# Second attention of a two-layer macaron block: which step turns the first half of the outputs, and which steps give ScalarE both score pairs

## The chip, the cores and the metric

The kernel runs on one core of one Trainium2 chip. The metric is device time in microseconds, from launch to end, as the median of three runs. All engines named are those of this core: TensorE (matmuls), VectorE, ScalarE, GpSimd, and SyncE, whose queue issues the DMAs.

## What is computed

Eight sequences of 512 tokens, 128 channels, pass through two layers of (half FFN, attention, half FFN). The stages in order are ffn0, attn0, ffn0, ffn1, attn1, ffn1. The change touches attn1 alone. There, with 16 heads of 8 channels:

```
qkv = x @ w_qkv;  q, k, v per head
w = relu(q k^T / sqrt(8))
attn = (w / (sum(w) + 1e-6)) @ v
y = x + attn @ w_out + b_out
x_new = x_in + layernorm(y) * gamma + beta
```

(the x of this formula is itself the layer norm of the running x_in.)

## The kernel before

**Tiling.** A chunk is one sequence of 512 tokens; each stage runs over eight chunks. Each engine has its own instruction stream, written out by hand as tables of steps, and the streams meet in semaphores. A body of an attn1 chunk has sixteen steps (slots). In each step an engine first does its tail steps for the chunk before, then its prep steps for the chunk after, then its main work of this chunk. What comes earlier in this order is ahead in the engine's queue.

**Main work.** Step n of attn1 handles four heads (quad n // 4) against one block of 128 keys (n % 4). TensorE (pe_attn1) makes two score pairs, m = 2n and 2n + 1. Each is two matmuls of 128 keys by 512 queries into the double bank pair[m % 3] (L818). A score pair must be read out before pair m + 3 may be written (taken_wait). The read-out is the ReLU into the ring probs. Even pairs are always ScalarE's (L944). Odd pairs are VectorE's (L1227), except in the steps of ACT_BOTH, where ScalarE does both. Of the 32 pairs of a chunk ScalarE does 21 and VectorE 11.

**Products.** PV n (pv1, L646) multiplies the four heads' weights of step n with the values and adds to bank 6. PV_AT says in which step it is issued, behind the scores: PV 7 in step 9, none in step 10, PV 8 to 12 in steps 11 to 15, and the last three in steps 0 and 1 of the next chunk. PVs 0 to 7 fill the first half of the outputs and PVs 8 to 15 the second.

**Taking a half out.** take_half (VectorE, L1146 to L1158) waits until the eight products of the half are done, turns bank 6 (a 32x32 block transpose), adds the epsilon, takes the reciprocal and multiplies. PV 8 (and PV 0 of the next chunk) waits for the turn. The first half is taken at the head of the step HALF_AT["attn1"], ahead of that step's ReLU; the second in step 2 of the next chunk.

**Tail of an attn1 chunk, run during the next.** VectorE: second half in step 2, fin in step 3, aT_lo in step 5. TensorE: proj in step 10 (twelve matmuls on bank 7). VectorE: y_norm in step 11 (L1257 to L1266, it waits for proj). GpSimd: y_rstd in step 12 (L1291). VectorE: y_scale in step 13 (L1271). GpSimd: y_add in step 14 (L1295 and L1298).

**Preparation of the next chunk.** In step 15 GpSimd does keep (L1284). In step 0 VectorE takes the layer norm's statistics (ending with ve, L967) and GpSimd makes rstd (L1279). In step 1 VectorE makes xn (L976), ahead of ReLU 3. In step 3 TensorE transposes xn (L544). GpSimd also copies the values of a quad into place (put_values, L1315, steps 2, 9, 10 and 15) and adds the bias row in step 10 (L1321).

The first chunk of attn1 has the tail of an ffn1 chunk in place of proj to y_add, and the last one prepares an ffn1 chunk, with the router's steps on VectorE and ScalarE.

Of the kernel before, what the change touches and what calls it, by code (L numbers as in the profile page):

```python
# [117 lines left out]
NPAIR = 3  # L118
NP1 = 2 * NS1
PV_AT = ((-3,), (-2, -1), (), (0, 1), (2,), (3,), (4,), (5,), (6,), (7,), (), (8,), (9,), (10,), (11,), (12,))  # L120
ACT_BOTH = (0, 2, 10, 11, 13)
HALF_AT = {"attn0": 13, "attn1": 10}
PUT_AT = {"attn0": (11, 13, 18, 3), "attn1": (9, 10, 15, 2)}
Q_FILLS = ((0, ((3, 0),)), (1, ((3, 0),)), (0, ((2, 0), (0, 384))), (1, ((2, 0), (0, 384))), (None, ((1, 0),)))
K_FILLS = ((0, ((0, 0),)), (1, ((0, 0),)), (0, ((1, P), (3, 0))), (1, ((1, P), (3, 0))), (None, ((2, 0),)))
# [11 lines left out]
def ring(use):  # L137

    what, n = use
    return (USES.index((what, n % NS0)) - (len(USES) if n < 0 else 0)) % NPAIR  # L140
# [49 lines left out]
def taken_by(m):  # L190

    return "act" if m % 2 == 0 or m // 2 in ACT_BOTH else "dve"

# [6 lines left out]
def build(nc, x_in, w0, w1, wa, biases, bd3, rows, consts, out, scratch, mixed):  # L200
    nc.disable_value_cache = True
    ctx = ExitStack()
    with ctx:
# [930 lines left out]
        def take_half(eng, ch, half):  # L1134

            mem, n = ch.mem, 2 * ch.ga + half
            if ch.causal:
                eng.wait_ge(pv0_done, 3 * (NQ * ch.g + 2 * half + 2))
                src = bank6
            else:  # L1140
                eng.wait_ge(pv1_done, ROUND + ch.g * NS1 + (2 * half + 2) * NT)
                src = bank6
            eng.wait_ge(attn_ready, n)
            if ch.causal and half:
                eng.wait_ge(x_done, ONE + ch.G)
            eng.transpose(mem.o_turn[:, :, :].rearrange("p n c -> p (n c)"), src[:, :]).then_inc(o_turned, 1)  # L1146
            eng.wait_ge(o_turned, n + 1)
            o = mem.o_turn[:, :, 0:2 * VC].rearrange("p n (g c) -> p n g c", c=VC)
            if ch.causal:
                eng.reciprocal(rden[:, 1, :, :], o[:, :, :, HD]).then_inc(rden_ready, 1)  # L1150
            else:
                eng.tensor_scalar(rden[:, 0, :, :], o[:, :, :, HD], KERN_EPS, None, ALU.add).then_inc(eps_added, 1)
                eng.wait_ge(eps_added, 2 * ch.g + half + 1)
                eng.reciprocal(rden[:, 1, :, :], rden[:, 0, :, :]).then_inc(rden_ready, 1)
            eng.wait_ge(rden_ready, n + 1)
            if half == 0:
                eng.wait_ge(aT_ready, ch.ga)
            eng.tensor_tensor(  # L1158
                mem.attn[:, :, 16 * half:16 * half + 16].rearrange("p n (g d) -> p n g d", d=HD), o[:, :, :, 0:HD],
                rden[:, 1, :, :].unsqueeze(3).broadcast_to([P, NBLK, 2, HD]), ALU.mult).then_inc(attn_ready, 1)  # L1160
# [13 lines left out]
        def maximum(eng, ch, f, b):  # L1174

            quad, fill, m = f // NF, f % NF, mem0
            k = ch.g * NS0 + f + 1
            q = m.rmax[:, quad % 2, :, :]
            src = pair[b]
            eng.wait_ge(s_ready, k)  # L1180
            heads = slice(0, QUAD) if fill == NF - 1 else slice(2 * Q_FILLS[fill][0], 2 * Q_FILLS[fill][0] + 2)
            if fill == NF - 1:
                eng.tensor_reduce(q[:, 1, :].rearrange("p (h b) -> p b h", b=2), src[:, :, :].rearrange("p b (h s) -> p b h s", h=2),  # L1183
                                  AX_X, ALU.max).then_inc(s_used, 1)
            elif len(Q_FILLS[fill][1]) == 1:
                eng.tensor_reduce(q[:, 3, heads], src[:, :, :], AX_X, ALU.max).then_inc(s_used, 1)
            else:
                eng.tensor_reduce(q[:, 2, heads], src[:, :, 0:384], AX_X, ALU.max)
                eng.tensor_reduce(q[:, 0, heads], src[:, :, 384:S], AX_X, ALU.max).then_inc(s_used, 1)
            if fill == NF - 1:  # L1190
                st = neg_max
                st.begin(NQ * ch.g + quad)
                eng.wait_ge(s_used, k)
                eng.wait_ge(mx_zeroed, 1)
                if quad or not ch.first:
                    eng.wait_ge(q_ps, NQ * ch.g + quad)
                mx_hi, mx_lo = (mx[:, :, :].rearrange("p t (h r) -> p t h r", r=PC)[:, :, :, NROW * HD + i] for i in range(2))
                v = st.mark(eng.tensor_scalar(mx_hi, q, -1.0, None, ALU.mult))
                eng.wait_ge(st.sem, v)
                st.mark(eng.scalar_tensor_tensor(mx_lo, q, -1.0, mx_hi.bitcast(F32), ALU.mult, ALU.subtract))  # L1200
                st.end()

        def dve_attn0(eng, ch, n):
# [9 lines left out]
            elif not ch.last:  # L1213
                maximum(eng, ch.after(), f - NS0, ring(("q", n)))
            if n == HALF_AT["attn0"]:
                take_half(eng, ch, 0)

        def dve_attn1(eng, ch, n):

            i = ch.g * NS1 + n  # L1220
            if n == HALF_AT["attn1"]:
                take_half(eng, ch, 0)
# [493 lines left out]
```

## Time and profile before

| | us |
|---|---|
| median of 3 runs | 2091.01 (2084.22 to 2091.42) |
| profiled execution, its own time | 2088.05 |
| its span, first to last instruction | 2086.0 |
| attn1 in that span | about 1440 to 1702 |

| engine | busy us | share of the span |
|---|---|---|
| TensorE matmul | 1991.1 | 95% |
| TensorE weight load | 1440.4 | 69% |
| VectorE | 1646.3 | 79% |
| ScalarE | 1198.4 | 57% |
| GpSimd | 929.6 | 45% |

The mean granted clock of TensorE is 0.984 of full speed. Ends of matmuls are modelled, so a busy TensorE isn't one at its peak. In the rows, PE is TensorE, DVE VectorE, ACT ScalarE, POOL GpSimd, and L12 is line 12 of the kernel.

### The profile page before, as it was taken

What the parts mean: (1) busy time and instruction counts of PE and PEld (TensorE: products, weight loads), DVE (VectorE), ACT (ScalarE), POOL (GpSimd) and SP (SyncE); (2) the same over time, 40 slices, a digit from 0 to 9 for tenths busy, and PEclk for the clock granted to TensorE, in tenths of its full rate; (3) what the DMA queues carried; (4) which work ended last, traced back from release to release, by engine and by line L of the source; (5) the groups of instructions that cost most, each with busy time, mean ns of one, the idle gap of its engine ahead of it and who ended that gap; (6) DMA issues with size and microseconds to landing.
All of it is one profiled execution on the core that took longest, in us unless ns stands there. A gap on an engine that the chain in (4) does not pass through costs nothing.

```text
span 2086.0 us, 44742 instructions
## 1 busy us (share of the span) xinstructions
PE 1991.1 (95%) x10752; PEld 1440.4 (69%) x10752; DVE 1646.3 (79%) x3337; ACT 1198.4 (57%) x1736; POOL 929.6 (45%) x904
## 2 busy tenths in 40 slices
PE   6999998999999889999999999998999999999998
PEld 4777776666666677777777888885333347787787
DVE  6777787777777577777768888886777788888887
ACT  6667664555555657667644444444767764445444
POOL 4655553233333356666634444442222235444444
PEclk9999999999999999999999999999999999999999
DMA  5333333333323134444401111113342411111112
GB/s 203 99 117 111 101 119 113 97 97 98 93 80 91 45 110 127 114 126 126 125 26 43 50 50 41 46 46 110 113 131 81 131 37 45 47 42 46 41 51 71
DMA packets 120701, 179.29 MB, mean 86 GB/s; under 512 B 33840, under 2 KB 38576, under 8 KB 120496
## 3 DMA queue, kind: packets, MB, share of 16 engines
q1 hardware_dynamic: 120624, 178.37, 28.9%
q8 instruction: 36, 0.59, 0.1%
q14 instruction: 41, 0.34, 0.0%
HBM read 147.10 MB, written 31.20 MB: 85 GB/s over the span
## 4 chain that ended last, share of the span: by engine, by line
PE 61%; DVE 12%; issue 12%; POOL 9%; ACT 3%; DVEq 1%; DMA 1%; SPq 1%; POOLq 1%; ACTq 0%
PE pair L392 13%; PE pair L394 12%; PE pair L393 12%; POOL h_lo L1358 6%; PE bank L646 4%; PE pair L735 3%; PE bank L624 3%; PE pair L757 3%; PE pair L818 2%; PE bank L392 2%; PE bank L394 1%; PE bank L393 1%; DVE rmax L1183 1%; DVE xn L976 1%; DVE h_hi L1126 1%
## 5 line engine op out<-in xcount | busy, mean ns | idle before, releaser
L1364 POOL TENSOR_TENSOR h_lo<-hid,h_hi 128x512 fp32r<-128x512 f32 x256 | 335.5, 1311 | 409.6 <-ACT h_hi L915 409.4
L1358 POOL TENSOR_TENSOR h_lo<-hid,h_hi 128x512 fp32r<-128x512 f32 x256 | 331.5, 1297 | 216.3 <-ACT h_hi L881 215.7
L392 PE MATMUL pair<-xnT_hi,w_hi 128*128 (+1 forms) x1040 | 420.4, 404 | 4.4 <-DVE prod L1105 3.0
L394 PE MATMUL pair<-xnT_hi,w_lo 128*128 (+1 forms) x1040 | 408.0, 392 | 0.0
L393 PE MATMUL pair<-xnT_lo,w_hi 128*128 (+1 forms) x1040 | 407.2, 392 | 0.0
L910 ACT ACTIVATE hid<-pair,bias 128x512 f32<-128x512 f32 x256 | 176.5, 689 | 315.7 <-PE pair L394 275.2
L392 PE MATMUL pair<-h_hi,w_hi 128*128 128x512 f32 x784 | 312.0, 398 | 14.4 <-DVE h_lo L1128 6.3
L394 PE MATMUL pair<-h_hi,w_lo 128*128 128x512 f32 x784 | 306.4, 391 | 0.0
L393 PE MATMUL pair<-h_lo,w_hi 128*128 128x512 f32 x784 | 306.2, 391 | 0.0
L1126 DVE TENSOR_SCALAR h_hi<-pair,nb 128x512 fp32r<-128x512 f32 x256 | 191.1, 746 | 70.3 <-PE pair L394 67.5
L881 ACT ACTIVATE h_hi<-hid 128x512 fp32r<-128x512 f32 x256 | 161.2, 630 | 140.6 <-DVE hid L1110 135.9
L1105 DVE SCALAR_TENSOR_TENSOR prod<-pair,bias,wb 128x512 f32<-128x512 f32 x256 | 190.7, 745 | 63.5 <-PE pair L394 47.5
L933 ACT ACTIVATE probs<-pair 128x1024 f32<-128x1024 f32 x160 | 163.4, 1024 | 130.0 <-PE pair L757 126.9
L392 PEld LDWEIGHTS pair<-xnT_hi,w_hi 128*128 128x128 f32 x1040 | 196.6, 189 | 48.0 <-DVE prod L1105 4.7
L394 PEld LDWEIGHTS pair<-xnT_hi,w_lo 128*128 128x128 f32 x1040 | 196.2, 189 | 42.8
L393 PEld LDWEIGHTS pair<-xnT_lo,w_hi 128*128 128x128 f32 x1040 | 197.0, 189 | 36.1
L1110 DVE TENSOR_TENSOR hid<-pair,prod 128x512 f32<-128x512 f32 x256 | 177.1, 692 | 55.0 <-DVE prod L1105 35.8
L1339 POOL TENSOR_SCALAR_AFFINE_SELECT probs<-probs 128x512 f32<-128x512 f32 (+1 forms) x160 | 86.9, 543 | 265.9 <-ACT probs L933 265.9
L1128 DVE SCALAR_TENSOR_TENSOR h_lo<-pair,nb,h_hi 128x512 fp32r<-128x512 f32 x256 | 192.3, 751 | 9.0
L944 ACT ACTIVATE probs<-pair 128x1024 f32<-128x1024 f32 x168 | 164.8, 1026 | 52.5 <-PE pair L818 45.7
L890 ACT ACTIVATE pair<-pair,bias 128x512 f32<-128x512 f32 x256 | 167.4, 654 | 43.8 <-PE pair L394 41.2
L392 PEld LDWEIGHTS pair<-h_hi,w_hi 128*128 128x128 f32 x784 | 147.6, 188 | 64.8 <-DVE h_lo L1128 12.6
(163 smaller groups left out, 3253.6 us busy)
## 6 DMA issues: line engine op xcount, KB each, us to landing
wb<-parts_dram SPq DMA_DIRECT2D x512, 128.0 KB, 2.9
wb<-parts_dram SPq DMA_DIRECT2D x128, 256.0 KB, 3.3
parts_dram<-attn_parts SPq DMA_DIRECT2D x96, 256.0 KB, 3.0
attn_q_st<-parts_dram SPq DMA_DIRECT2D x64, 256.0 KB, 2.7
k_one<-parts_dram SPq DMA_DIRECT2D x128, 64.0 KB, 2.5
attn_k_st<-parts_dram SPq DMA_DIRECT2D x32, 256.0 KB, 3.1
stage_w<-in_w_dram SPq DMA_DIRECT2D x32, 130.0 KB, 2.5
stage_w<-in_w_dram SPq DMA_DIRECT2D x5, 512.0 KB, 5.8
```

What stands on the lines that cost most here:

```text
L392: eng.matmul(o, w_hi_, v_hi, start=start, stop=False, **kw)
L393: eng.matmul(o, w_hi_, v_lo, start=False, stop=False, **kw)
L394: return eng.matmul(o, w_lo_, v_hi, start=False, stop=stop, **kw)
L890: eng.activation(gate_bank(p)[:, :], gate_bank(p)[:, :], ACT.Silu, bias=bias[:, b:b + 1]).then_inc(silu_ready, 1)
L910: eng.activation(hid[:, i % NHID, :], unit_bank(j)[:, :], ACT.Relu, bias=bias[:, B1 + j:B1 + j + 1]).then_inc(hid1_ready, 1)
L944: eng.activation(probs[:, n % PRING, 2 * (m % 2):2 * (m % 2) + 2, :], pair[m % NPAIR][:, :, :], ACT.Relu).then_inc(p1_ready["act"], 1)
L1105: eng.scalar_tensor_tensor(prod[:, p % 2, :], bank[2 + p % 2][:, :], bias[:, b:b + 1], wb[:, i % NWB, :], ALU.add, ALU.mult).then_inc(prod ...
L1110: eng.tensor_tensor(hid[:, i % NHID, :], gate_bank(p)[:, :], prod[:, p % 2, :], ALU.mult).then_inc(hid_ready, 1)
L1126: eng.tensor_scalar(h_hi[:, j % NH1, :], unit_bank(j)[:, :], floor, None, ALU.max).then_inc(hi1v_ready, 1)
L1128: eng.scalar_tensor_tensor(h_lo[:, j % NH1, :], unit_bank(j)[:, :], floor, h_hi[:, j % NH1, :].bitcast(F32), ALU.max, ALU.subtract).then_i ...
L1358: eng.tensor_tensor(h_lo[:, p % NH0, :], hid[:, unit_of(p) % NHID, :] if p else hs[:, :], h_hi[:, p % NH0, :].bitcast(F32), ALU.subtract). ...
L1364: eng.tensor_tensor(h_lo[:, j % NH1, :], hid[:, j // 2 % NHID, :], h_hi[:, j % NH1, :].bitcast(F32), ALU.subtract).then_inc(lo1p_ready, 1)
```

## The change

```diff
-ACT_BOTH = (0, 2, 10, 11, 13)
-HALF_AT = {"attn0": 13, "attn1": 10}
+ACT_BOTH = (0, 2, 9, 11, 13)
+HALF_AT = {"attn0": 13, "attn1": 9}
```

In step 9 ScalarE does the ReLUs of pairs 18 and 19, where VectorE did 19. In step 10 VectorE does the ReLU of pair 21, which ScalarE did. VectorE takes the first half of the outputs at the head of step 9, where it did so at the head of step 10. Both lines hold for all eight chunks of attn1, and for nothing else.

## Rows read from the trace of the kernel before

**Rows 1.** Timeline, VectorE, turns of second halves: start us, us, instruction, [idle before <-releaser]
```profile
1576.85 0.71 DVE L1146 STREAM_TRANSPOSE attn_o_turn<-bank 128x512 f32<-128x512 f32 x1
...
1611.13 0.70 DVE L1146 STREAM_TRANSPOSE attn_o_turn<-bank 128x512 f32<-128x512 f32 x1
...
1643.19 0.70 DVE L1146 STREAM_TRANSPOSE attn_o_turn<-bank 128x512 f32<-128x512 f32 x1
```

**Rows 2.** Stretches of the fourth chunk: length; busy us (instructions) per engine; PEclk; DMA share; GB/s
```profile
1557.10:1560.50 3.40, 2.91 (x26) 1.71 (x18) 2.90 (x6) 1.19 (x2) 0.48 (x2) 1.00 0.60 190
1560.50:1567.30 6.80, 6.40 (x30) 1.41 (x34) 4.09 (x15) 4.56 (x6) 1.38 (x2) 0.54 0.41 136
```

**Rows 3.** Timeline, TensorE, sixth chunk, PV 7 to score pairs 28 and 29
```profile
1625.39 1.06 PE L646 MATMUL bank<-probs,attn_v_st 128*32 128x512 f32 x8
...
1627.87 0.73 PE L818 MATMUL pair<-attn_q_st,attn_k_st 24*128 24x512 f32 x6
1629.49 0.50 PE L818 MATMUL pair<-attn_q_st,attn_k_st 24*128 24x512 f32 x2 [0.89 <-ACT probs L944]
...
1630.92 0.90 PE L818 MATMUL pair<-attn_q_st,attn_k_st 24*128 24x512 f32 x4
...
1632.75 0.91 PE L818 MATMUL pair<-attn_q_st,attn_k_st 24*128 24x512 f32 x4
...
1634.58 0.50 PE L818 MATMUL pair<-attn_q_st,attn_k_st 24*128 24x512 f32 x4
```

**Rows 4.** Timeline, ScalarE, runs of ReLUs in the sixth, the first and the last chunk
```profile
1628.41 4.69 ACT L944 ACTIVATE probs<-pair 128x1024 f32<-128x1024 f32 x5 [2.21 <-PE pair L818]
...
1462.10 4.69 ACT L944 ACTIVATE probs<-pair 128x1024 f32<-128x1024 f32 x5 [0.35 <-PE pair L818]
...
1689.10 5.70 ACT L944 ACTIVATE probs<-pair 128x1024 f32<-128x1024 f32 x6
```

**Rows 5.** Timeline, VectorE, sixth chunk, ReLU 19 to y_scale
```profile
1625.50 1.22 DVE L1227 TENSOR_SCALAR probs<-pair 128x1024 f32<-128x1024 f32 x1 [0.48 <-PE pair L818]
1626.64 0.70 DVE L1146 STREAM_TRANSPOSE attn_o_turn<-bank 128x512 f32<-128x512 f32 x1
...
1628.08 0.43 DVE L1158 TENSOR_TENSOR attn_attn<-attn_o_turn,rden 128x256 f32<-128x256 f32 x1
1628.81 0.69 DVE L1257 TENSOR_TENSOR attn_xk<-bank,attn_xk 128x512 f32 x1 [0.30 <-issue]
...
1631.14 0.17 DVE L1266 TENSOR_SCALAR y_ve<-y_mv 128x4 f32<-128x4 f32 x1
1631.87 1.23 DVE L1227 TENSOR_SCALAR probs<-pair 128x1024 f32<-128x1024 f32 x1 [0.56 <-PE pair L818]
1633.01 1.20 DVE L1271 TENSOR_SCALAR attn_xk<-attn_xk,y_mv,y_rstd  x4
```

**Rows 6.** Chain of waits, sixth chunk into the seventh: start us, us, piece
```profile
1631.87 0.71 DVE probs L1227
...
1634.59 1.29 POOL attn_xk L1295
...
1639.57 1.02 POOL rstd L1279
...
1642.06 1.23 DVE probs L1227
...
1644.12 1.92 PE bank L646 x16
```

**Rows 7.** Timeline, VectorE, end of the statistics and xn in the seventh chunk
```profile
1639.31 0.17 DVE L967 TENSOR_SCALAR ve<-mv 128x4 f32<-128x4 f32 x1
...
1640.94 1.20 DVE L976 TENSOR_SCALAR xn<-x,mv,rstd 128x128 f32 x4 [1.46 <-POOL rstd L1279]
```

**Rows 8.** Timeline, GpSimd, sixth chunk: value copy after PV 7, y_rstd
```profile
1626.66 0.31 POOL L1315 COPY attn_v_st<-attn_v_tok 128x128 f32<-128x128 f32 x1 [0.80 <-PE bank L646]
...
1631.39 1.02 POOL L1291 TENSOR_TENSOR y_rstd<-y_ve,mhalf 128x4 f32<-128x4 f32 x1 [4.42 <-DVE y_ve L1266]
```

## The prediction

> **What bounds the kernel now.** I read the page first. TensorE is busy for 95% of the span, so a change pays only through TensorE's own waits. The edit touches only the second attention (span time 1440 to 1702 us, eight chunks of sixteen steps), so the other 1824 us stay as they are, and the chunk is the thing to look at. The timeline gives its length: the second-half turn of the outputs (L1146) starts at 1576.85, 1611.13 and 1643.19 [rows 1], so one chunk took 34.28 us and the next 32.06 us for the same work. The table of stretches says why: in the long chunks the granted clock went from 1.00 to about half (2.4 to 1.2 GHz) for 6.8 us, and just before that TensorE had been busy 2.91 of 3.40 us with small matmuls and short waits [rows 2]. This happened in the middle of the fourth and the fifth chunk, for a shorter time in the first, and in the middle of no other. A fall costs 34.28 - 32.06 = 2.2 us.
>
> Then an undisturbed chunk, the sixth, engine by engine around the edited steps. On TensorE [rows 3] the last product of the first half, PV 7, starts at 1625.39. The output projection follows, and score pairs 20, 21 and 22 start at 1627.87. Pair 23 then waits 0.89 us for ScalarE: its banks are freed by the ReLU of pair 20. Twice more, at 1630.92 and 1632.75, the four score matmuls take 0.90 us; unheld, as at 1634.58, they take 0.50. The reason is ScalarE [rows 4]: it is idle for 2.21 us, then does five ReLUs in a row (pairs 20 to 24) in 4.69 us, 0.94 each, and TensorE walks behind them. VectorE [rows 5] does ReLU 19, turns the half (L1146 to L1158, 1626.64 to 1628.51), then y_norm (L1257 to L1266), ReLU 25, and y_scale (L1271) from 1633.01.
>
> The last view is the chain of waits [rows 6], and it decides the case. It doesn't stay on TensorE: it runs from ReLU 25 to y_scale, to GpSimd's y_add from 1634.59, through GpSimd's queue (the rest of y_add, keep, a copy, rstd L1279 at 1639.57), to VectorE's xn and ReLU 3 (1642.06), and so to the first products of the next chunk at 1644.12. VectorE's own way to rstd ends with ve at 1639.48 and is a tie with it [rows 7]. So two paths bound the chunk: TensorE after ScalarE in steps 10 to 12, and VectorE then GpSimd from step 10 to step 3 of the next chunk. The second ends last.
>
> **The change part by part.** ScalarE has 21 ReLUs and VectorE 11 per chunk, before and after. Only pairs 19 and 21 change places, and the turn goes ahead of step 9's ReLU slot. No work or DMA is added, and the stack transfers keep their waits.
>
> *The turn.* It can't begin before PV 7 is done. GpSimd's copy (L1315), which waits for the same count, starts at 1626.66, and the turn now starts at 1626.64 [rows 5, 8]. PV 7's record ends at 1626.45 [rows 3], so the moved turn starts at 1626.5 to 1626.64. It gains 0 to 0.14 us; I take 0.10, since the turn already starts as close to the end of a product as the copy does. Nothing is queued behind it that could use the gain: VectorE idles from the end of ReLU 17 to that point instead of doing ReLU 19. PV 8, which waits for the turn, starts at 1629.9, far after the turn.
>
> *Pair 19 to ScalarE.* It fits into the 2.21 us idle: 0.94 us, done at about 1627.1. Pair 22, which needs those banks, starts after 1627.87. Cost nothing; if the idle were not there, 0.94 us.
>
> *Pair 21 to VectorE.* This shortens ScalarE's row to 20, 22, 23. Pair 23 still waits the same 0.89 us for 20. Pair 25 no longer waits for 22 (0.90 becomes 0.5) and pair 27 waits less: TensorE reaches PV 10 about 0.7 us earlier (0.4 + 0.3). But ReLU 21 stands in VectorE's queue ahead of y_norm. The turn ends at 1628.4, pair 21 is written by then, and the ReLU takes 1.22 us, to about 1629.65. y_norm starts there and not at 1628.81: 0.8 us later, or 1.1 if the 0.30 us of issue time before it stays. That moves ve of y_norm to 1631.94, GpSimd's y_rstd from 1631.39 to 1632.2 [rows 8], and y_scale to 1632.2 + 1.37, the 1.37 being from the start of rstd to the start of xn (1639.57 to 1640.94) [rows 6, 7]. That is 1633.6, against 1633.01 now: 0.6 us later (0.9 at the other bound). ReLU 25 then ends at about 1633.3 and is not last.
>
> *Where it goes.* y_add, keep, rstd, xn, ReLU 3 and the next chunk's first product each follow without slack, so all move by 0.6. The tie with ve falls to GpSimd's side: TensorE's 0.7 us ends in a longer wait at step 3. What is late next is rstd in GpSimd's queue. This passage exists six times, from the second to the eighth chunk. In two of the six the clock fell, TensorE was last, rstd waited for ve, and at half clock TensorE doesn't wait for ScalarE, so neither the loss nor the gain counts: 4 x 0.6 = 2.4 us.
>
> *First and last chunk.* The first has no projection, and ScalarE's idle time before pair 20 is only 0.35 us [rows 4]; ReLU 19 pushes 20 by about 0.5 us, and pair 23 with it. In the last there is no gap at all (six in a row, 5.70 us [rows 4]); 20 comes up to 0.9 us later, and half of that is won back because 22 is next. I take 0.5 + 0.3 = 0.8 us, bounds 0 to 1.4.
>
> *Sum.* 2.4 + 0.8 = 3.2 us on the profiled execution's 2088.05 us (span 2086.0 and 2.05 around it): 2091.3 us. The three runs were 2084.22, 2091.01 and 2091.42; the profiled one lies 3 us below their median, and the mean of the four is 2088.7. Falls of the clock, one more or one less, are enough for that scatter, so I add the sum to the mean: 2091.9 us. Bounds of the terms: 4 x 0 + 0 to 6 x 0.9 + 1.4, thus 0 to 6.8 us.
>
> **The rivals.**
> *A, TensorE's gain comes through.* If the passage through y_norm and GpSimd has slack that the chain of waits doesn't show (it is a tie within 0.1 us), the 0.7 us stay won: 6 x 0.7 = 4.2 us less, 2084.5 us. For it: the broken row of five ReLUs is real. Against it: VectorE sat idle for rstd (1.46 us before xn [rows 7]), so xn moves with it.
> *B, the clock (slower).* The wait moves from steps 11 and 12 to step 3 of the next chunk. There TensorE has only a transpose and four score matmuls to do, and the wait grows from about 0.7 us in three pieces to about 1.9 us. The stretch before a fall in the trace had only 0.49 us idle of 3.40 [rows 2], so this one may well bring falls at a place where there was none. Price: 2.2 us each as traced, at most 3.4 (6.8 us at half speed with nothing to absorb it). It decides from five extra falls at 2.2 or three at 3.4; one or two give 2094 to 2099, all six 2105 to 2112.
> The Trainium skill, TensorE: Matmul & The Clock Gate, has two rules on this. Its table "Why this matters for your kernels" ties falls to long idle gaps between bursts; by that none would occur here before or after, B would be void, and the time would be the 2091.9 us of the sum. Its "A second HAM failure mode: psum-queue depth-cycling" says that frequent small idles between matmul groups are enough to make the clock swing; by that B holds, up to its 2112 us. The trace agrees with the second: the longest single wait before the fall in the fourth chunk was 0.89 us.
> *C, nothing.* If ReLU 21 slips in with no delay of y_scale (lower bounds), the time is 2088.7 within 1 us.
>
> **How the numbers follow.** The delay that passes on: 0.55. A: 0.15. B: 0.20. C: 0.10. The predicted time is 2091.9. A median of few runs moves by 3 us with the falls that happen to be in it: so 2091.9 less 7 for A and a run with few falls gives 2085; upward, B with two to three extra falls gives 2100. A measurement of this kernel can tell 0.5% (10.5 us) from no change. Faster by more needs A and several falls fewer: 0.03. Slower by more needs the upper third of B: 0.07. The rest, 0.90, is within 0.5%.
>
> **What would show it.** In an undisturbed chunk of the changed kernel: the turn 1.2 us before score pair 20; ScalarE in runs of two or three ReLUs, pair 25 unheld; y_norm starting 1.7 us after pair 20 where it is 0.9 now; rstd waiting for GpSimd's own queue and no longer in a tie; a chunk of 32.6 to 32.7 us. Falls of the granted clock near the first products of a chunk would show B. If the undisturbed chunk is 31.4 us, A is right, and my reading of the chain through GpSimd is wrong. If y_norm isn't later, the order on VectorE isn't what I think.

## The result

The changed kernel takes 2097.47 us (median of 11 runs, 2092.82 to 2101.93), the kernel before 2088.86 us beside it (11 runs, 2081.66 to 2094.50). The ratio is 1.0054, with a 95% interval of 1.0042 to 1.0066: slower by 0.54%, some 11 us by this ratio and 8.6 us by the two medians, where 3 us were forecast. The time lies in the stated range (2085 to 2100), but the middle of the forecast was 6 us too low, and the loss sits at the edge of the 0.5% to which "same" had been given 0.90.

The profiled execution of the changed kernel took 2097.0 us, with a span of 2095.1 us. Busy times have hardly moved, and the mean granted clock is 0.981 (0.984 before):

```profile
span 2095.1 us, 44741 instructions
...
PE 1994.7 (95%) x10752; PEld 1439.7 (69%) x10752; DVE 1653.9 (79%) x3337; ACT 1199.4 (57%) x1736; POOL 929.3 (44%) x904
```

**The edited steps, in the third chunk.** First the part that came as forecast. On VectorE (timeline; start, us, instruction, idle before it), which answers to [rows 5]:

```profile
1528.13 0.72 DVE L1146 STREAM_TRANSPOSE attn_o_turn<-bank 128x512 f32<-128x512 f32 x1 [1.61 <-PE bank L646]
...
1529.97 1.23 DVE L1227 TENSOR_SCALAR probs<-pair 128x1024 f32<-128x1024 f32 x1
1531.11 0.68 DVE L1257 TENSOR_TENSOR attn_xk<-bank,attn_xk 128x512 f32 x1
...
1533.44 0.17 DVE L1266 TENSOR_SCALAR y_ve<-y_mv 128x4 f32<-128x4 f32 x1
```

The turn waits 1.61 us for PV 7, ReLU 21 follows it, and y_norm (L1257) comes behind both. Score pair 20 starts at 1529.38 here (the first of the TensorE rows below), so y_norm is 1.73 us behind it; before it was 0.94 us (1627.87 to 1628.81 [rows 3, 5]). On ScalarE the row of five ReLUs [rows 4] is broken as intended: three in a row, and 1.30 us idle ahead of them. On TensorE the change buys nothing at pair 23:

```profile
1529.92 2.85 ACT L944 ACTIVATE probs<-pair 128x1024 f32<-128x1024 f32 x3 [1.30 <-PE pair L818]
```
```profile
1529.38 0.73 PE L818 MATMUL pair<-attn_q_st,attn_k_st 24*128 24x512 f32 x6
1531.00 0.50 PE L818 MATMUL pair<-attn_q_st,attn_k_st 24*128 24x512 f32 x2 [0.89 <-ACT probs L944]
```

**The next chunk's start.** This is the part that was mis-weighed. TensorE in steps 0 to 3 of the fourth chunk (timeline):

```profile
1540.99 1.92 PE L646 MATMUL bank<-probs,attn_v_st 128*32 128x512 f32 x16
1542.85 0.51 PE L818 MATMUL pair<-attn_q_st,attn_k_st 24*128 24x512 f32 x4
1544.54 0.65 PE L544 MATMUL bank<-ident,xn 128*128 128x128 f32 x4 [1.18 <-DVE xn L976]
1545.45 0.58 PE L818 MATMUL pair<-attn_q_st,attn_k_st 24*128 24x512 f32 x4 [0.26 <-DVE probs L1227]
1546.25 3.44 PE L646 MATMUL bank<-probs,attn_v_st 128*32 128x512 f32 x16 [0.21 <-DVE attn_o_turn L1146]
```

The wait for xn is now 1.18 us. In the undisturbed chunk of the kernel before, the same transposes came almost without one:

```profile
1642.41 0.65 PE L544 MATMUL bank<-ident,xn 128*128 128x128 f32 x4 [0.17 <-issue]
```

The first two products of the changed kernel (L646 x16, 1546.25) take 3.44 us, where sixteen matmuls of the same line took 1.92 us at 1540.99. The table of stretches, before and after the fall in two successive chunks (columns as in [rows 2]), shows why:

```profile
1507.90:1511.30 3.40, 1.95 (x20) 0.71 (x12) 2.50 (x6) 2.17 (x3) 0.85 (x2) 1.00 0.00 0
1511.30:1514.70 3.40, 3.20 (x20) 0.79 (x20) 3.17 (x6) 1.91 (x3) 0.00 (x0) 0.58 0.00 0
1541.90:1545.40 3.50, 2.11 (x20) 0.72 (x12) 2.35 (x6) 2.23 (x4) 1.10 (x2) 1.00 0.00 0
1545.40:1548.80 3.40, 3.14 (x16) 0.89 (x20) 3.17 (x6) 2.08 (x3) 0.00 (x0) 0.58 0.00 0
```

TensorE was busy for 1.95 us of 3.4 and 2.11 us of 3.5 with light work, and the clock went from 2.4 to 1.2 GHz for 3.4 us just when the dense products began. It did so at 1511, 1545, 1580, 1614 and 1682 us. Besides, it fell for 6.8 us in the middle of the sixth chunk (1635 us) and of the first (1464 us, where the kernel before has a fall of 3.4 us). The second-half turns of the changed kernel, which answer to [rows 1]:

```profile
1478.37 0.71 DVE L1146 STREAM_TRANSPOSE attn_o_turn<-bank 128x512 f32<-128x512 f32 x1
...
1511.06 0.71 DVE L1146 STREAM_TRANSPOSE attn_o_turn<-bank 128x512 f32<-128x512 f32 x1
...
1545.32 0.70 DVE L1146 STREAM_TRANSPOSE attn_o_turn<-bank 128x512 f32<-128x512 f32 x1
...
1579.48 0.70 DVE L1146 STREAM_TRANSPOSE attn_o_turn<-bank 128x512 f32<-128x512 f32 x1
```

The one undisturbed chunk is 32.69 us long (forecast: 32.6 to 32.7). The next ones are 34.26 and 34.16 us. A fall at this place costs 34.2 - 32.7 = 1.5 us in these chunks.

**Stage by stage.** The whole difference is in attn1. All lengths in us, each from one profiled execution, from second-half turn to second-half turn. The two columns "filled" are experiments 7 and 8 below, whose traces show no fall of the clock in attn1 but the one at its beginning; the last column is their difference.

| piece | before | changed | before, filled | changed, filled | filled pair |
|---|---|---|---|---|---|
| first score pair to first such turn | 38.79 | 40.70 | 37.54 | 38.58 | +1.04 |
| second chunk | 32.31 | 32.69 | 32.32 | 32.74 | +0.42 |
| third | 32.07 | 34.26 | 32.06 | 32.67 | +0.61 |
| fourth | 34.31 | 34.16 | 32.08 | 32.68 | +0.60 |
| fifth | 34.28 | 34.16 | 32.07 | 32.68 | +0.61 |
| sixth | 32.06 | 35.60 | 32.04 | 32.69 | +0.65 |
| seventh | 31.70 | 33.25 | 31.69 | 33.25 | +1.56 |
| last | 27.73 | 29.13 | 27.73 | 28.26 | +0.53 |
| sum | 263.25 | 273.95 | 257.53 | 263.55 | +6.02 |

The attn1 of the two kernels differs by 10.7 us, that of the filled pair by 6.0. Of the 6.0, 0.57 us lies between the first score pair and PV 7 of the first chunk, where the edit has not acted yet: this stretch took 21.04 and 21.61 us in the filled pair, 21.14 and 21.28 in the two kernels, and 22.34 in experiment 11. So the edit's plain waits are about 5.4 us, and the other 5 us are the clock, as it fell in these two executions.

The two don't simply add. After the fall in the middle of the sixth chunk TensorE was so late that it found xn ready in the seventh; there it had neither the wait nor a fall at the first products:

```profile
1648.47 0.65 PE L544 MATMUL bank<-ident,xn 128*128 128x128 f32 x4 [0.16 <-issue]
```

The stages ahead of attn1 happened to be 1.7 us shorter in the profiled execution of the changed kernel, which is why the spans differ by 9.1 only.

### The profile page after: what moved, and what is told of

The parts are those of the page before. It is cut to its first block, busy times and chain, and to the rows that moved or that the text cites. A ratio compares the mean times of both kernels' runs of the same rounds, so it can differ in the third digit from the quotient of the medians.

```text
span 2095.1 us, 44741 instructions
## 1 busy us (share of the span) xinstructions
PE 1994.7 (95%) x10752; PEld 1439.7 (69%) x10752; DVE 1653.9 (79%) x3337; ACT 1199.4 (57%) x1736; POOL 929.3 (44%) x904
## 4 chain that ended last, share of the span: by engine, by line
PE 59%; DVE 13%; issue 12%; POOL 9%; ACT 3%; DVEq 2%; SPq 1%; POOLq 1%; DMA 1%; ACTq 0%
PE pair L392 12%; PE pair L394 12%; PE pair L393 12%; POOL h_lo L1358 6%; PE bank L646 4%; PE pair L735 3%; PE bank L624 3%; PE pair L757 3%; PE pair L818 2%; PE bank L392 2%; PE bank L394 1%; PE bank L393 1%; DVE rmax L1183 1%; DVE prod L1105 1%; DVE xn L976 1%
```

## The experiments

**1. Only ScalarE's steps changed.**

```diff
-ACT_BOTH = (0, 2, 10, 11, 13)
+ACT_BOTH = (0, 2, 9, 11, 13)
```

> The kernel before with ACT_BOTH at steps 0, 2, 9, 11, 13 and the turn left at step 10. Theory Q (what matters is the order of VectorE's queue): VectorE has no ReLU in step 9, so the turn still stands directly ahead of ReLU 21, as in the changed kernel. The time is that of the changed kernel, 2097 us, about 0.4% over before, with undisturbed chunks of 32.7 us. Rival T (the earlier turn has a part in it): the turn is a step later and the time lies between, 2090 to 2094 us.

Measured: 2097.62 us, ratio 1.0054 (1.0041 to 1.0067), the same as the changed kernel; undisturbed chunks of 32.68 and 32.66 us. VectorE has nothing else to do between the old place of the turn and the new one, so the order of its work is the same with the turn at step 9 or 10. Rival T is out: moving the turn does nothing once the ReLUs have changed places.

**2. Only the turn moved.**

```diff
-HALF_AT = {"attn0": 13, "attn1": 10}
+HALF_AT = {"attn0": 13, "attn1": 9}
```

> The kernel before with the turn at step 9 and ACT_BOTH untouched: VectorE waits for PV 7, turns, and then does ReLU 19; ScalarE does 20 and 21. Theory Q: y_norm is again behind one turn and one ReLU, so 0.8 us later after PV 7 than before, and pair 22 waits for ReLU 19 until about 1.8 us after pair 20 is due; the row of ReLUs on ScalarE is held up too. An undisturbed chunk of 32.7 to 33.5 us, the time 2096 to 2102 us. Rival T: the earlier turn is what costs, and this kernel is as slow as the changed one, 2097 us, with the same chunks.

Measured: 2094.26 us, ratio 1.0040 (1.0027 to 1.0053). Chunks are 32.6 to 34.5 us long, most of them with a fall of the clock in them; the sixth, without one, is 32.58. The turn now has ReLU 19 behind it, and costs by that. The direction is as theory Q has it; its time was set 2 us too high and its chunk 0.1 us too long, and rival T's 2097 us were not met either.

**3. Both ReLUs on ScalarE.**

```diff
-ACT_BOTH = (0, 2, 9, 11, 13)
+ACT_BOTH = (0, 2, 9, 10, 11, 13)
```

> The changed kernel with ReLU 21 on ScalarE as well (ACT_BOTH 0, 2, 9, 10, 11, 13): VectorE does neither 19 nor 21. Theory Q: y_norm starts 0.9 us after pair 20 again (1.7 in the changed kernel), undisturbed chunks are back at 32.0 to 32.1 us, and the time is that of before within 2 us (2087 to 2091 us), although the turn is at step 9 and ScalarE has one ReLU more. Rival S (the loss is ReLU 19 on ScalarE, which fills the gap in which it could wait for pair 20): the loss stays, 2095 us or more.

Measured: 2092.31 us, ratio 1.0027 (1.0016 to 1.0038). Neither expectation was met. In the middle of the stage theory Q holds: the chunks without a fall are 32.30, 32.16, 32.17 and 31.80 us, as before. But the ends stay long: 40.69 us to the first turn and 30.7 us for the last chunk, against 38.79 and 27.73. ScalarE has no idle time there, and both pieces have a fall of the clock of 6.8 us in them (at 1465 and 1694 us); this led to the next two.

**4 and 5. The middle and the ends apart.** The table of ScalarE's steps depends on the chunk: in the first kernel the new one (with the turn at step 9) holds for the second to seventh chunk, in the other for the first and the last.

```diff
+ACT_BOTH_NEW = (0, 2, 9, 11, 13)
+def is_new(ch):
+    return not (ch.first or ch.last)
...
-    return "act" if m % 2 == 0 or m // 2 in ACT_BOTH else "dve"
+    return "act" if m % 2 == 0 or m // 2 in (ACT_BOTH_NEW if new else ACT_BOTH) else "dve"
...
-            if n == HALF_AT["attn1"]:
+            if n == (9 if is_new(ch) else 10):
```

> Second to seventh chunk as in the changed kernel, first and last chunk as before. Theory M (the loss is made where ReLU 21 delays y_norm, which happens in the middle chunks, and by the clock falls that this brings): most of the loss is here, 6 to 8 us over before, 2093 to 2095 us. Rival E (the loss is made at the ends, where ScalarE has no idle time to take ReLU 19): within 3 us of before.

Measured: 2092.60 us, ratio 1.0027 (1.0016 to 1.0038).

> First and last chunk as in the changed kernel, the six between as before. Theory M: 1 to 4 us over before (the two traced chunks were longer by 1.9 and 1.4 us, falls of the clock in them included), 2088 to 2090.5 us. Rival E: 6 us or more over before.

Measured: 2090.78 us, ratio 1.0019 (1.0007 to 1.0031). The two add up to 0.46% of the 0.54%. The middle has more of the loss, but less than theory M said (5.6 us in place of 6 to 8), and the two end chunks have 0.19%, about 4 us (0.07 to 0.31%, thus 1.5 to 6.5 us), which is near the top of what was expected and over the 0.8 us of the prediction. It isn't all waiting: in the trace of this kernel the clock fell for 6.8 us in the first chunk, where the kernel before has 3.4 us. In the first chunk of the changed kernel pairs 22 and 23 wait 0.42 us each for ScalarE, and pair 24 waits 0.34 us for ReLU 21, which is behind the turn on VectorE; before, pair 23 alone waited, for 0.71 us. That makes 0.47 us more:

```profile
1461.16 0.49 PE L818 MATMUL pair<-attn_q_st,attn_k_st 24*128 24x512 f32 x2 [0.42 <-ACT probs L944]
1462.08 0.50 PE L818 MATMUL pair<-attn_q_st,attn_k_st 24*128 24x512 f32 x2 [0.42 <-ACT probs L944]
1462.51 1.06 PE L646 MATMUL bank<-probs,attn_v_st 128*32 128x512 f32 x8
...
1463.91 0.73 PE L818 MATMUL pair<-attn_q_st,attn_k_st 24*128 24x512 f32 x4 [0.34 <-DVE probs L1227]
```

**6. The wait at step 3 filled.** The changed kernel, with four matmuls of which nothing is used, ahead of the transpose that waits for xn:

```diff
             if step == "turn":
+                if ch.kind == "attn1" and not ch.first:
+                    eng.wait_ge(v_ready, ch.ga)
+                    eng.wait_ge(x_done, ONE + ch.G - 2)
+                    for _ in range(4):
+                        eng.matmul(bank7[:, :], wa_hi[:, 1, 0, :], xnT_hi[:, 0, :], start=True, stop=True)
                 eng.wait_ge(ln_steps.sem, ch.G * 13 + 13)
```

> The changed kernel with four added matmuls (128x128 by 128x512, result thrown away, bank 7) in the wait of TensorE ahead of the transpose of step 3. They take about 0.9 us of a wait of 1.15 us. Theory C (the greater part of the loss is the clock, which falls because the wait was moved to step 3): no fall near the first products of a chunk, chunks of 32.7 us where 34.2 was traced, and 4 to 6 us less than the changed kernel, 2091 to 2093 us; falls in the middle of a chunk may remain. Rival W (the loss is the longer waits alone and the falls come with any schedule): the falls stay, the time is 2097 us or a little more.

Measured: 2092.38 us, ratio 1.0023 (1.0011 to 1.0036), 5 us less than the changed kernel. In its trace the third, fifth and sixth chunk are 32.72, 32.70 and 32.67 us, where 34.2 was the rule; falls remain in the middle of the second and fourth chunk, in the last, and near the first products of the last (where the fill isn't, since it prepares an FFN chunk). Theory C is borne out in time and place: added work there makes the kernel faster. Rival W's 2097 us is out.

**7 and 8. The wait ahead of pair 23 filled.** Three unused matmuls into bank 6, in the wait of 0.89 us, ahead of PV 8; once in the kernel before, once in the kernel of experiment 6:

```diff
             for h in range(2):
                 m = 2 * n + h
+                if m == 23:
+                    eng.wait_ge(o_turned, 2 * ch.ga + 1)
+                    for _ in range(3):
+                        eng.matmul(bank6[:, :], wa_hi[:, 1, 0, :], xnT_hi[:, 0, :], start=True, stop=True)
```

> The kernel before with three added matmuls (128x128 by 128x512, result thrown away, bank 6, after the turn and ahead of PV 8) in the wait of 0.89 us ahead of score pair 23. Theory C (falls of the clock in the middle of a chunk come from this wait): no falls in the middle of the chunks, undisturbed chunks of 32.1 us throughout, 3 to 5 us less than before, 2082 to 2084 us, and less scatter. Rival W (the falls have another cause, or matmuls on the full array are no help): same time as before or some 1 to 2 us more.

Measured: 2080.45 us (2076.34 to 2082.93), ratio 0.9964 (0.9950 to 0.9978). It beats both kernels, and by 1.6 us also the range that was expected. In its trace every chunk from the third to the sixth is 32.04 to 32.08 us long, and the clock falls nowhere in the stage but at its beginning. The first of the second-half turns:

```profile
1472.81 0.71 DVE L1150 STREAM_TRANSPOSE attn_o_turn<-bank 128x512 f32<-128x512 f32 x1
...
1505.13 0.70 DVE L1150 STREAM_TRANSPOSE attn_o_turn<-bank 128x512 f32<-128x512 f32 x1
...
1537.19 0.70 DVE L1150 STREAM_TRANSPOSE attn_o_turn<-bank 128x512 f32<-128x512 f32 x1
```

> The changed kernel with both fills: four added matmuls ahead of the transpose of step 3, three ahead of pair 23. Theory C: no falls in the middle chunks at all, each 32.7 us, and a time of before plus the plain delay of 0.6 us in six chunks, less the falls that before has: 2085 to 2089 us. That is 2 to 5 us under the same kernel with the first fill alone (2092.4 us). Rival W: no better than that one.

Measured: 2087.73 us, ratio 1.0001 (0.9988 to 1.0014), chunks of 32.67 to 32.74 us (the seventh 33.25) and, in the trace, again no fall after the stage's beginning. The traces of this pair take the clock out of the comparison and give the 5.4 us of plain waits worked out above. The medians differ by 7.3 us, but that isn't waits alone. The two profiled executions are among the fastest of their kernels (2078.18 and 2083.39 us, 5.2 us apart), with a mean granted clock of 0.992 and 0.993. The other executions go down to 0.989 and 0.987, so the clock falls in some of them; no trace shows where.

**9. The delay alone.** The kernel of experiment 7, with two memsets of unused tiles on VectorE ahead of y_norm; no ReLU and no turn is moved:

```diff
             if step == "y_norm":
                 st = tail
                 st.begin(ch.g)
+                eng.memset(mixed_sb[:, :], 0.0)
+                eng.memset(xnT_lo[:, 1, :].bitcast(F32), 0.0)
```

> The kernel before with the fill ahead of pair 23 (2080.5 us, no falls), and two memsets of unused tiles on VectorE ahead of y_norm: 2 x 0.49 us traced, of which 0.2 to 0.3 fall into issue time that is there anyway, so y_norm is 0.7 to 0.8 us later. No ReLU and no turn is moved. Theory Q and C: this alone makes undisturbed chunks of 32.6 to 32.9 us, and falls of the clock of 3.4 us come near the first products of the chunk, where this kernel had none; 2087 to 2092 us. Rival: if the moved ReLUs themselves matter (ScalarE's row, the banks), the chunks stay near 32.1 us and there are no falls, 2081 to 2083 us.

Measured: 2086.07 us, ratio 0.9992 (0.9981 to 1.0003), thus 5.6 us more than with the fill alone; the time was expected 1 us higher at least. The chunks are what both theories said: 32.70 and 32.57 us undisturbed, then 34.20, 34.21 and 34.21 us, with falls at 1537, 1571, 1605 and 1640 us. The stretches around the first of them:

```profile
1533.60:1537.00 3.40, 2.48 (x24) 1.01 (x16) 2.77 (x6) 2.16 (x4) 0.58 (x2) 1.00 0.00 0
1537.10:1540.50 3.40, 3.20 (x20) 0.61 (x16) 3.17 (x7) 1.99 (x3) 0.00 (x0) 0.61 0.00 0
```

So a delay of y_norm by itself makes the longer chunk and brings the falls to the first products. This is the experiment that shows the mechanism; the others fit it. It also shows its limit: one chunk earlier TensorE waited for xn too (0.77 us), was busy for about as much of the stretch, 2.51 us of 3.40, and no fall followed. The added wait lets the falls in, but what decides which passage has one stays open.

```profile
1500.50:1503.90 3.40, 2.51 (x24) 0.83 (x16) 2.20 (x5) 2.15 (x3) 1.17 (x2) 1.00 0.00 0
```

**10. Less work on GpSimd.** The kernel of experiment 7, with the multiplication by gamma moved from GpSimd to VectorE:

```diff
+                eng.wait_ge(tail.sem, v)
+                eng.tensor_tensor(xk, xk, row_of(2), ALU.mult).then_inc(y_scaled, 1)
...
-                eng.wait_ge(tail.sem, 13 * ch.g + 13)
                 xk = attn1_xk[:, ch.parity, :, :]
-                eng.tensor_tensor(xk, xk, row_of(2), ALU.mult).then_inc(y_scaled, 1)
```

> The kernel before with the fill ahead of pair 23, and the multiplication by gamma moved from GpSimd (1.28 us and 0.5 us of gap behind it) to VectorE (0.69 us). The result is the same. If the way through GpSimd bounds the chunk together with VectorE's statistics in a tie, as read in the chain of waits, TensorE's path and ve take over at once: chunks of 31.8 to 32.1 us, 2078 to 2081 us, at most 0.1% less than with the fill alone. If GpSimd alone bounds it: up to 0.6 us less per chunk, 31.5 us, 2077 us. If VectorE is the bound, the added 0.69 us show: 2083 us or more.

Measured: 2081.62 us, ratio 0.9971 (0.9957 to 0.9984): no difference from the fill alone that can be told, and chunks of 32.04 to 32.08 us. The way did become shorter: at the start of the seventh chunk GpSimd is ready 0.72 us early and waits for VectorE's ve, which is where it was relative to TensorE's products:

```profile
1629.24 1.02 POOL L1285 TENSOR_TENSOR rstd<-ve,mhalf 128x4 f32<-128x4 f32 x1 [0.72 <-DVE ve L971]
```

The way through GpSimd is in a tie with the others, as the chain of waits and [rows 7] had it: lengthened it costs all, shortened it gives nothing.

**11. The seventh chunk.** From the kernel with both fills; GpSimd's row add of the last chunk is held back:

```diff
                 eng.wait_ge(ln_steps.sem, ch.G * 13 + 13)
+                if ch.kind == "attn1" and ch.last:
+                    eng.wait_ge(pv1_done, ROUND + ch.g * NS1 + 4)
```

> The changed kernel with both fills, and GpSimd's row add of the last chunk held back until that chunk's PV 3, so that it can't run beside VectorE's xn. Theory P (in the last chunk xn takes 2.07 us in place of 1.12 because the two run side by side): xn is back at about 1.1 to 1.2 us, and the time from second-half turn to second-half turn into the last chunk falls from 33.25 us to 32.3 us. Rival: xn is slow there for another reason, 2.07 us and 33.25 us stay. The whole time moves by less than it can be measured to.

Measured in one profiled execution: xn is back at 1.12 us, and the piece is 32.29 us long in place of 33.25. Theory P holds. The lines of VectorE and GpSimd in the kernel with both fills, and VectorE's of this one:

```profile
1666.72 2.07 DVE L985 TENSOR_SCALAR xn<-x,mv,rstd 128x128 f32<-128x128 f32 x4 [1.28 <-POOL rstd L1288]
```
```profile
1667.44 1.26 POOL L1330 TENSOR_TENSOR x<-x,row 128x512 f32<-128x512 f32 x1
```
```profile
1669.01 1.12 DVE L985 TENSOR_SCALAR xn<-x,mv,rstd 128x128 f32<-128x128 f32 x4 [1.28 <-POOL rstd L1288]
```

## Why the prediction was right and wrong

**Right: what bounds the chunk, and the delay.** TensorE and ScalarE in steps 10 to 12 and VectorE with GpSimd behind them are in a tie, ReLU 21 stands ahead of y_norm, the delay goes through to the next chunk's first products, and TensorE's 0.7 us is lost in a longer wait. In the filled pair the passage cost 0.60 to 0.65 us in four chunks (0.42 in the second), forecast 0.6. y_scale starts 5.71 us behind pair 20 in the changed kernel's third chunk, before 5.14 us. TensorE's three waits at step 3 are 1.65 us together (1.18, 0.26 and 0.21), before 0.64 us; about 1.9 was forecast. The turn did gain nothing. Rival A is out (experiments 9 and 10), rival C too.

**Wrong: "4 x 0.6", the plain waits of the passages.** This is the first step that failed: the filled pair shows 4.45 us in the six passages where the sum has 2.4. Two of the six were counted as free because the clock had fallen in the middle of these chunks in the one trace at hand. The reason given holds: a chunk with such a fall hides the delay (0.16 us of wait at 1648 in the changed kernel). But this was so in one passage of the changed kernel, not in two, and in none of the filled pair. How many falls there are differs between executions of one kernel: the mean granted clock of the kernel before goes from 0.981 to 0.989. Where they lie differs between kernels: in the fourth and sixth chunk in experiment 3, in the second and fourth in experiment 6, though in experiment 5 again in the fourth and fifth.

**Wrong: the passage into the last chunk.** Of those 4.45 us it alone has 1.56. GpSimd has no further chunk to prepare there, comes to its row add early, and runs it beside the xn that the edit has made late (experiment 11). The prediction took all six passages as alike. With the row add held back this passage costs 32.29 - 31.69 = 0.60 us.

**The ends: the size right, a part of the reason not seen.** 0.8 us was forecast. In the filled pair the first chunk costs 0.47 us from PV 7 on (16.50 and 16.97 us to the second-half turn) and the last 0.53, thus 1.0 us. That pair 24 of the first chunk would wait for ReLU 21 was not seen: in the middle chunks the projection gives VectorE the time, in the first there is none. The 4 us of experiment 5 have falls of the clock in them.

**Wrong: the clock counted as nothing in the sum.** This is the second step that failed, and it weighs as much as the first. The falls of the clock were described in rival B, at the right place and by the mechanism that experiment 9 shows, and given 0.20; in the sum of 3.2 us they have no term. They came at five of the six passages. The price of one was too high: 1.5 us each was traced, not 2.2, since only 3.4 us at half speed follow, and B is to be set against the falls that the kernel before has anyway. In all the clock makes about 5 us of the 10.6 between the two traces. Plain waits of 5.4 us in place of 3.2, and some 5 us of clock on top, made the loss; either alone would have left the kernel within 0.5%. B should not have been a rival to the sum but a term of it: the stretch ahead of a fall in [rows 2] was busier (2.91 of 3.40 us) than the one that the edit was about to make (1.95).

**Luck.** That the time still lies inside 2085 to 2100 is owed to the upper bound, which had been set by two to three extra falls at 2.2 us, and not to the sum.

The Trainium skill's two rules in TensorE: Matmul & The Clock Gate come out as the first trace had them, with the second ahead. By the table in "Why this matters for your kernels", only long gaps matter; but in the traces of the two kernels no wait ahead of a fall, the stage's beginning left out, is longer than 1.53 us (the wait for xn ahead of the fall at 1682), and most are 0.9 to 1.2 us. By "A second HAM failure mode: psum-queue depth-cycling", frequent small idles are enough, and the traces of experiments 6 to 9 agree.

## What to carry to other kernels

When two paths are in a tie, work taken off one gives nothing and work put ahead of the other costs in full: look up in the chain of waits what is queued behind an instruction before moving it there. A wait of TensorE can have a second price, in the clock, where its work is light. Put that price into the sum and not beside it, and where the wait can't be removed, try to fill it with matmuls that nobody needs (7 us here, 0.36%). And what one trace shows of the clock in one chunk need not be a property of that chunk.

## What was not expected of the hardware

**Short VectorE instructions beside GpSimd's.** In five of the changed kernel's chunks, from the second on, ve on VectorE, 128x4 elements and 0.17 us in [rows 7], takes 1.05 to 1.10 us. It falls beside GpSimd's keep (1.28 us). Timeline of both engines, end of the second chunk's work (the statistics for the next):

```profile
1505.95 1.28 POOL L1284 TENSOR_TENSOR attn_xk<-xn,row 128x512 f32 x1 [0.25 <-DVE mv L965]
```
```profile
1506.16 1.10 DVE L967 TENSOR_SCALAR ve<-mv 128x4 f32<-128x4 f32 x1
```

It ends as keep does (1507.26 and 1507.23), and the xn of 2.07 us in experiment 11 ends as the row add beside it does (1668.79 and 1668.70). This reads as standing still until GpSimd is done, not as being slowed in proportion. The Trainium skill says so in SBUF — State Buffer, section "SBUF: two separate sides": VectorE in certain modes and GpSimd exclude each other at a shared port for the whole instruction. The trace agrees with the exclusion; in which mode ve runs it doesn't show.

**The falls keep step.** In the changed kernel and in experiment 9 the clock fell near the first products in four successive chunks, some 34.2 us apart, where the undisturbed length is 32.7 us. The row ends in the changed kernel with the fall in the middle of the sixth chunk, after which the wait for xn is gone, and in experiment 9 at the last chunk. That a fall lengthens the chunk by just as much as keeps the next in place is a reading that no experiment here has tested.

**The fill isn't a cure everywhere.** In experiment 11 one fall of 6.8 us remained in the last chunk, at 1688 us, with the fill in place; at the stage's beginning all kernels have one. What tells these from the others stays open.
